# Output projection of a group inside its fourth sample's step on TensorE, with constant products in five more waits of the stage

## What is computed

```
xn = _layernorm(x, gamma1, beta1)
qf = elu(xn @ W_q_lin + b_q_lin) + 1.0
kf = elu(xn @ W_k_lin + b_k_lin) + 1.0
vl = xn @ W_v_lin + b_v_lin
lin_out = qf @ (kf.T @ vl) / (qf @ kf.sum(0) + 1e-06)
...                                    # win_out: windowed attention, an earlier stage
gate_in = concatenate([lin_out, win_out, xn], axis=-1)
gate = sigmoid(relu(gate_in @ W_g1 + b_g1) @ W_g2 + b_g2)
fused = gate * lin_out + (1.0 - gate) * win_out
h = h + fused @ W_out + b_out
...
z = einsum('nd,sdr->nsr', _layernorm(h), P)        # feed-forward, routing
scores = einsum('nsr,smr->nsm', z, C)
topv, topi = top_k(scores, 4)                      # softmax weights of the 4 best of 64, for 8 sets
```

## Time and profile before

| what | us |
|---|---|
| median of 3 runs | 1776.65 |
| lowest and highest run | 1770.56, 1781.34 |
| the profiled execution, its own time | 1772.55 |
| its span, first to last instruction | 1770.8 |
| the stage of the change, from its first product to the last before the next stage | about 880 to 1087 of the span |
| PE, DVE, ACT, POOL busy over the whole span | 91%, 56%, 42%, 32% |

### The profile page before, as it was taken

How to read it: one execution, slowest core, us unless ns; L and a number is a source line. 1 busy time by engine, 2 the same in 40 slices (tenths; PEclk the granted TensorE clock), 3 DMA queues, 4 the chain that set the end, 5 groups by cost and what they waited for, 6 DMA issues and landing times. The chain is left out here.

```text
span 1770.8 us, 36202 instructions
## 1 busy us (share of the span) xinstructions
PE 1616.4 (91%) x13700; PEld 1108.4 (63%) x13700; DVE 986.9 (56%) x2745; ACT 737.1 (42%) x1424; POOL 574.4 (32%) x547
## 2 busy tenths in 40 slices
PE   8999799999996999979888887999998999889996
PEld 5677589976654899756555453222225775558886
DVE  3487722236858222268536765888886767932221
ACT  1266223324541111135424555999993553211110
POOL 1231122225411342365001224555552101324553
PEclk8999789999996999989999978999999999999998
DMA  6000455521005455212100117999990004026662
GB/s 233 1 2 2 177 168 181 179 89 30 18 2 209 160 182 179 74 26 95 51 14 20 44 51 263 404 385 362 353 324 28 2 2 159 1 87 182 195 192 31
DMA packets 97459, 228.24 MB, mean 129 GB/s; under 512 B 24297, under 2 KB 55753, under 8 KB 96393
## 3 DMA queue, kind: packets, MB, share of 16 engines
q1 hardware_dynamic: 77527, 206.14, 33.1%
q0 software_dynamic: 19552, 19.63, 4.6%
q10 hardware_dynamic: 210, 0.15, 0.0%
HBM read 198.91 MB, written 26.56 MB: 127 GB/s over the span
## 5 line engine op out<-in xcount | busy, mean ns | idle before, releaser
L2984 ACT ACTIVATE l2s_hidden<-ps,pack_l2f 128x816 f32<-128x816 f32 x256 | 227.1, 938 | 17.1 <-PE ps L2908 7.6
L3003 POOL TENSOR_TENSOR l2s_gated<-l2s_hidden,l2s_whole 128x408 f32<-128x408 f32 x128 | 136.9, 1070 | 102.0 <-PE ps L2916 102.0
L117 PE MATMUL ps<-pack_const 128*128 128x512 bf16 x596 | 150.5, 402 | 10.5 <-PEq L2324 5.1
L3026 DVE TENSOR_TENSOR l2s_gated<-l2s_hidden,l2s_whole 128x816 f32<-128x816 f32 x128 | 142.6, 1114 | 27.7 <-ACT l2s_hidden L2984 26.0
L2483 POOL DMA_INDIRECT l_xt<-rows_in,l_tokens x66 | 63.2, 957 | 244.2 <-PE ps L2496 187.2
L2524 PE MATMUL ps<-l_down,l_hidden 128*128 x792 | 139.9, 326 | 0.0
L2524 PEld LDWEIGHTS ps<-l_down,l_hidden 128*128 128x128 f32 x792 | 127.3, 190 | 0.5 <-issue 0.3
L117 PEld LDWEIGHTS ps<-pack_const 128*128 128x128 bf16 x596 | 58.1, 102 | 82.6 <-issue 30.1
L2507 PE MATMUL ps<-l_xtT,l_up 128*128 128x128 f32 x792 | 99.5, 275 | 3.4 <-DVE l_xtT L2759 3.4
L2507 PEld LDWEIGHTS ps<-l_xtT,l_up 128*128 128x128 f32 x792 | 96.7, 192 | 4.5 <-DVE l_xtT L2759 4.5
L2603 ACT ACTIVATE l_hidden<-ps,l_down 128x128 f32<-128x128 f32 x198 | 55.2, 375 | 89.6 <-PE ps L2512 89.5
(11 more groups left out here) (585 smaller groups left out, 3564.8 us busy)
## 6 DMA issues: line engine op xcount, KB each, us to landing
l2s_whole<-g_whole SPq DMA_DIRECT2D x128, 612.0 KB, 7.4
l_up<-in_l_up SPq DMA_DIRECT2D x66, 576.0 KB, 3.8
l3c_wg<-in_l_gate SPq DMA_DIRECT2D x16, 576.0 KB, 4.9
l3c_wu<-in_l_up SPq DMA_DIRECT2D x16, 576.0 KB, 6.5
l3c_wd<-in_l_down SPq DMA_DIRECT2D x16, 576.0 KB, 3.8
slots_out<-l_y SPq DMA_DIRECT2D x66, 96.0 KB, 2.3
l_down<-in_l_down SPq DMA_DIRECT2D x8, 675.0 KB, 9.3
l_down<-in_l_down SPq DMA_DIRECT2D x8, 576.0 KB, 7.5
```

What stands on the lines that cost most here:

```text
L117: pe.matmul(bank, halves[:, 0:128], halves[:, :], start=True, stop=True)
L2984: act.activation(hidden[:, p % kept, :, :], ps[:, 0, 2 * (p % 2):2 * (p % 2) + 2, 0:NG], ACT.Gelu_apprx_tanh, bias=w.at("b1")[:, s * MT + ...
L3003: pool.tensor_tensor(gated[:, (4 * n + 1) % ring, :], hidden[:, 2 * n % kept, 1, :], whole[:, n % ahead, 0, :], ALU.mult).then_inc(late_re ...
L3026: dve.tensor_tensor(gated[:, at:at + 2, :], hidden[:, (2 * n + 1) % kept, :, :], whole[:, n % ahead, 1:3, :], ALU.mult).then_inc(gated_rea ...
```

## The change

It edits TensorE's program alone. `step` takes an optional group, and issues that group's `out_products` between the scores (and first halves) and the wait for `zT_ready`; the fourth step of a loop round passes the group, and the separate call behind it is gone. The constant products grow: 9 new ones ahead of `lin_scores(0)`, behind a new wait for `v_ready`; 8 new ones in `mix_transposes` of the last group; 4 new ones ahead of `fused_transposes` of groups 1 to 3, behind a wait for `gate_in`; and 18 in place of 10 at the start of steps 8 and 12. That is 9 + 8 + 12 + 16 = 45 more. The other engines' programs are unchanged.

```diff
--- before.py
+++ after.py
@@ -1756,6 +1756,9 @@
                 last.then_inc(v_ps, 1)
 
             def lin_scores(q):
+                if q == 0:
+                    pe.wait_ge(v_ready, 1)
+                    fill(pe, g, ps[:, 1, 1, :], 9)
                 pe.wait_ge(lin_f_ready, q + 1)
                 pe.wait_ge(v_ready, q + 1)
                 if q:
@@ -1814,6 +1817,8 @@
                         if q + 1 < G:
                             pe.wait_ge(lin_x_ready, 4 * (q + 2))
                         hidden_wide(q, MIX)
+                        if q == G - 1:
+                            fill(pe, g, ps[:, 1, 1, :], 8)
                         pe.wait_ge(mixT_ready, MIX * q + 1)
                     for b in range(GB):
                         into = ps[:, 0, n % 2, b * L:(b + 1) * L]
@@ -1855,9 +1860,8 @@
 
             def fused_transposes(q):
 
-                if q == 0:
-                    pe.wait_ge(gate_in, q + 1)
-                    fill(pe, g, ps[:, 0, 0, :], 10)
+                pe.wait_ge(gate_in, q + 1)
+                fill(pe, g, ps[:, 0, 0, :], 4 if q else 10)
                 pe.wait_ge(fused_ready, q + 1)
                 for b in range(GB):
                     last = pe.transpose(ps[:, 0, 0, b * L:(b + 1) * L], gate[:, b, 0:WIDE], ident[0:L, 0:L])
@@ -1897,11 +1901,11 @@
                                      start=True, stop=True, tile_position=(0, 64 * (c % 2)))
                 last.then_inc(share_ps, 1)
 
-            def step(t):
+            def step(t, between=None):
                 biased, shared = (t - 6) // GB if t % GB == 2 else -1, (t - 8) // GB if t % GB == 0 else -1
                 if 0 <= t < B:
                     if t % GB == 0 and t // GB + 2 >= G:
-                        fill(pe, g, ps[:, 1, 1, :], 10)
+                        fill(pe, g, ps[:, 1, 1, :], 18)
                     pe.wait_ge(z_ready, t + 1)
                     if t:
                         pe.wait_ge(z1_left, t)
@@ -1918,6 +1922,8 @@
                     bias_products(biased, 0)
                 if shared >= 0:
                     shares(shared, 0)
+                if between is not None:
+                    out_products(between)
                 if 0 <= t < B:
                     pe.wait_ge(zT_ready, t + 1)
                     for c in range(C):
@@ -1964,9 +1970,7 @@
                 step(at[2])
                 if 1 <= q <= G:
                     fused_transposes(q - 1)
-                step(at[3])
-                if 1 <= q <= G:
-                    out_products(q - 1)
+                step(at[3], q - 1 if 1 <= q <= G else None)
             for t in range(B, LAST):
                 step(t)
 
```

## The result

The changed kernel takes 1781.01 us (median of 20 runs, 1773.82 to 1793.67) against 1776.55 for the kernel before (20 runs, 1765.83 to 1785.02). The ratio is 1.0042 with a 95% interval of 1.0025 to 1.0059, so it is slower by 4.4 to 10.5 us, 7.5 by the ratio and 4.5 by the medians.

The account below looks back on a forecast made before the run. No engine is full: the stage is a chain hopping between engines, mostly on TensorE, with gaps and half clock behind them. Terms -1.3 - 0.2 + 1.7 + 1.7 + 1.9 = +3.8 gave 1780.5 us, range 1767 to 1791.

Parts of the forecast that it names:

- The nine products: Ahead of round 0's first scores: they end 0.7 us behind the features but hold the clock, worth 2.0; -1.3 us.
- The projection does not fill the wait: Fourth step: projection waits for ScalarE's fused-row copies, so starts only 0.3 us before the wait for z's copy would end.
- Group 1: Step 3: only TensorE's own end counts, as its next work is independent of h; same duration, earlier start, -0.2 us.
- Group 2: Step 7: projection of z starts 2.3 us later, VectorE's remainder slips 1.7, and add_up with it; +1.7 us.
- Group 3: Step 11: same slip, less add_up's earlier wait of 1.29; +0.5 at full clock, +3.0 at half, middle +1.7 us.
- The mix: Last mix: eight products where TensorE had no gap, so nothing hides them; +1.9 us, twice that at half clock.
- the clock behind the gap at step 8: Eighteen products for ten at steps 8 and 12: nearly the same gap left, clock falls as before; 0 us.
- a clock of 1.0 there: Sign of a wrong forecast: granted clock of 1.0 in the stretch behind step 12 in the profile after.
- the first rival: Whole stage: clock holds and low stretches by steps 8 and 12 return 1.7 and up to 4.8; 1771.0 us, chance 0.18.
- the free move: Groups 2 and 3: VectorE's remainder does not set add_up, so the move costs nothing there; +0.4, 1777.1 us, chance 0.17.
- The one in which the clock holds: Same as the first rival: clock holds through the stage; -5.7 us, 1771.0, chance 0.18.
- The one in which the low clock falls onto the projection: Steps 3, 7 and 11: moved projection at half clock, +1.5, +5.0 and +3.0; +14.0 in all, 1790.7 us, chance 0.15.

Follow-up runs that it names:

- e1: The kernel before with only the output projection moved into the fourth step, no constant products added; ratio to before 1.0047.
- e7: The kernel before with only group 1's output projection moved into its fourth step; ratio to before 1.0003.
- e6: The kernel before with the output projection in the fourth step but behind the projection of z, no products added; ratio to before 1.0011.
- e2: The change with the output projection back behind the step, all 45 added products kept; ratio to before 0.9971.
- e8: e2 without the eight products in the last mix, so added products only and no move; ratio to before 0.9962.
- e4: The change with 40 products in the last group's mix in place of eight; 1792.90 us, ratio to before 1.0118.
- e3: The change without the eight products in the last group's mix; 1778.06 us, ratio to before 1.0025.
- e9: The kernel before with 18 constant products in place of 10 at steps 8 and 12, nothing else; ratio to before 0.9977.
- e10: e8 with 22 products for 18, and VectorE's add_up and statistics placed ahead of the last choice; ratio to before 0.9987.
- e5: The change without the mix products and with 30 constant products for 18 at steps 8 and 12; ratio to before 0.9999.

## Why the prediction was right, and where its terms were off

The forecast was slower, 1780.5, and the time is 1781.0. The agreement of the two numbers is in part luck: the sum was +3.8, the medians differ by 4.5 and the ratio says 7.5, between 4.4 and 10.5. So the sum lies just under the interval. In the pair of profiles the stage is 9.8 longer, and that splits at the z transposes into -0.3 up to step 0, nothing from there to step 3, +1.2 from step 3 to 4, +1.8 from 4 to 8, +7.7 from 8 to 12 and -0.6 behind. The terms missed in both directions.

The nine products: -1.3 forecast. From round 0's first product to the outputs' release of the next projection it is 17.5 before and 15.7 after, -1.8, more than the sum, which had left out L1771. But the gain did not last: at step 0's transposes, 52.6 and 52.3 from the same start, it is 0.3, with a low stretch in the change at 916 to 924. Over all traces no gain can be seen: 52.3 on average in the seven kernels with the nine and in the five without, with single ones from 50.8 to 53.8. The prediction took a gain at one place for a gain at the end.

The projection does not fill the wait: right at steps 3 and 7. It started with ScalarE's copy there, and 1.36 of the wait of 1.58 stayed in e1. At step 11 of the change TensorE was late by itself and the projection followed the scores, 0.7 behind the copy.

Group 1, -0.2: right as far as it was counted. It is 38.0 before and 37.9 after between the projections of groups 2 and 3, though the other kernels spread from 37.7 to 40.0 there, with the move and without, and e7 has 39.0. e7 alone is 1.0003. What was not counted is that the low clock of step 3 ran on over the projection of xn, whose first row took 2.96 for 1.64; that is the +1.2 from step 3 to 4.

Group 2, +1.7: right, +1.8, by the named path: the remainder with its wait of 1.81 and `add_up` without one. e6 shows that this place is the cause, as it puts the same products behind L1924 and 7 to 8 stays as it was. (The prediction calls them 12 products; the order lists show eight. No term hangs on it.)

Group 3, +1.7, the middle of 0.5 and 3.0: the middle was wrong and the full-clock price about right. VectorE needs 0.2 more at step 11 in the change and 0.4 more in e1, where the projection ran at full clock. Before, then e1:

```profile
1039.97 0.18 DVE L2204 COPY l2b_kept<-l2b_best 102x32 f32<-102x32 f32 x1
...
1048.24 0.67 DVE L2190 TENSOR_SCALAR x<-h,l2b_moments,l2b_rstd 102x192 f32<-102x192 f32 x2 [1.12 <-POOL l2b_rstd L1703]
```

```profile
1047.77 0.18 DVE L2204 COPY l2b_kept<-l2b_best 102x32 f32<-102x32 f32 x1
...
1056.45 0.67 DVE L2190 TENSOR_SCALAR x<-h,l2b_moments,l2b_rstd 102x192 f32<-102x192 f32 x2 [1.12 <-POOL l2b_rstd L1703]
```

It is small only because before the clock was low there and `add_up` stood 1.29 for TensorE. Against e2 and e8, where it was full and nothing was moved, the move costs 1.6. In the change, the row of the remainder at step 11 has a wait of 1.58 for ScalarE:

```profile
1048.24 0.27 DVE L2214 TENSOR_TENSOR pack_l0a<-ps,l2b_z_parts 128x102 f32<-128x102 f32 x1 [1.58 <-ACT l2b_z_parts L2056]
...
1051.02 1.01 DVE L2177 TENSOR_TENSOR h<-h,ps 102x384 f32<-102x384 f32 x2
```

The mix, +1.9: the mechanism is right, by e4 to the hundredth; the size was 2.8, because the products fell into half clock.

**The largest term that was mis-sized is the clock behind the gap at step 8**, which the sum put at 0 on the ground that nearly the same gap is left. The gap was indeed nearly the same (3.09 for 2.87), but the clock stayed low behind it for sixteen microseconds and not four. From step 8 to 12 e3, which has no products in the mix, is still 4.9 over before, and the slip at step 11 is 0.2 of that. It is not the amount of half clock but its place: the stage's mean is 0.91 for 0.89, and over all runs the granted clock of the change is 0.953 for 0.952. From step 8 to 11 TensorE took 35.4 at a mean of 0.71 against 26.9 at 0.89. Behind step 12 the opposite happened. The prediction had named a clock of 1.0 there as a sign that it was wrong, and the clock was 1.0, although the gap ahead was longer (3.36 for 2.15). That part took 37.6 for 38.3, so the sign came true and brought 0.6 us in place of the up to 4.8 that the first rival had priced.

How much of the 4.9 belongs to the change is not shown: e7 lost 5.9 us in the same stretch with no change in it. What many runs show is the other side. Products that shorten the gaps, without the move, raise the granted clock to 0.957 to 0.960 (e2, e8, e9, e10) and bring some 4 to 7 us (e9, e2, e8; 2 in e10 with VectorE's other order), and with the move in place e5 gains the like over e3. The eighteen products, taken as 0, would have been such a gain, and the move took it back by keeping the gap. Where the 3 to 4 us between the sum and the ratio lie stays open; the intervals of e1 to e9 are 3 to 6 us wide from end to end, so no finer split of the whole time is shown.

Of the rivals, the free move is out by e1. The one in which the clock holds was not the outcome, but e2 and e8 show its gain once the move is out. The one in which the low clock falls onto the projection did happen in part in step 3 (953 to 964 at 0.69) and did not in steps 7 and 11.

## What to carry to other kernels

A wait in front of an instruction is worth filling only with work whose own input comes clearly before that instruction's: look at what stands ahead of the releaser in the releasing engine's queue. And ask who waits for the instruction that is pushed back; here 2.6 us of products ahead of a small projection moved ScalarE, VectorE's queue and the next group by 1.8. Constant products paid in this kernel in the gaps of 2.2 to 3.4 us at steps 8 and 12, where TensorE's work follows at once (e5, e9). In the gap of 2.5 us of round 0 they showed no gain at step 0, and where TensorE had no gap they cost their full duration.

## What the runs showed of the hardware that I had not expected

How long the clock stays low behind a gap is not told by the gap. Behind 2.87 us the stretch at 1.2 GHz was 4 us long before, and in e7, with the same instructions and 2.86 us, the whole 45.6 us from step 8 to 12 had a mean clock of 0.71. In the change, the 3.09 us ahead of step 8 were followed by 16 us at 0.57, and the 3.36 us ahead of step 12 by none:

```profile
1055.37:1066.00 10.63, 8.24 (x47) 4.78 (x48) 8.16 (x58) 6.36 (x19) 3.06 (x4) 1.00 0.09 26
```

The Trainium skill (TensorE: Matmul & The Clock Gate, What's actually happening) says that the chip's watching of activity runs freely and does not start with the kernel, so that the same kernel sees a different number of slow matmuls from run to run. The traces here agree: e7 and the kernel before have the same instructions behind step 8, and 45.6 and 39.7 us for them. The clock goes with the spread of whole runs as well. Of the 20 runs of the change the fastest (1773.82) had a mean granted clock of 0.958 and the slowest (1793.67) 0.948, and the others lie nearly in the same order.
